# Normalised tiles written in bf16 and transposed in bf16, in the first norm stage of an attention and recurrent-FFN kernel

## The reference

```python
# attention, 16 heads of 64
h = layernorm(x)
q, k, v = h @ w_q, h @ w_k, h @ w_v            # split into heads; q and k are scaled by 1/sqrt(64) each
out = softmax(causal(dot)) @ v
x = x + layernorm(out @ w_u + b_u)
# FFN: a gated recurrence over the first axis (16 steps), then an output layer
c = sigmoid(xt wf + c uf + bf) * c + sigmoid(xt wi + c ui + bi) * tanh(xt wc + c uc + bc)   # xt = layernorm(x)[t]
x = x + layernorm(tanh(xt wo + c_final uo + bo))
```

## Time and profile before

| | us |
|---|---|
| three timed runs | 6600.88, 6709.1, 7143.36 (median 6709.1) |
| the profiled execution | 6599.17 |
| its span on the slowest core | 6597.6 |
| spans of the 8 cores | 6581.2 to 6597.6 |
| granted TensorE clock, mean of a core | 0.781 to 0.786 of full speed |

### The profile page before, as it was taken

The page is one execution under the profiler, slowest core; times in us unless marked ns, Lnnn a source line. Parts: engine busy times, 40 slices in busy tenths (PEclk is TensorE's granted clock), DMA queues, the critical chain, the costliest instruction groups (busy, mean ns, idle before and its releaser), DMA issues.

```text
span 6597.6 us, 85333 instructions; the slowest of 8 cores (6581.2 to 6597.6 us)
## 1 busy us (share of the span) xinstructions
PE 4671.3 (71%) x31972; PEld 2957.2 (45%) x31972; DVE 2211.4 (34%) x4162; ACT 1415.6 (21%) x2602; POOL 486.9 (7%) x399
## 2 busy tenths in 40 slices
PE   4877868686877868686877868687833323999954
PEld 2444444444444444444444444444511113888821
DVE  2232423233232423323242423323222233333378
ACT  1222130413222130413222130413200012222200
POOL 3010100101010100101010100101000011000022
PEclk8878878787878878787887868787855555999976
DMA  5010110101010110101010110101012232000044
GB/s 109 1 61 3 59 40 22 62 1 61 1 61 3 60 45 17 62 1 61 1 61 5 57 52 11 61 1 61 1 61 70 70 115 102 14 14 14 10 148 156
DMA packets 95071, 299.15 MB, mean 45 GB/s; under 512 B 14800, under 2 KB 14800, under 8 KB 94672
## 3 DMA queue, kind: packets, MB, share of 16 engines
q1 hardware_dynamic: 90000, 285.30, 13.1%
q0 software_dynamic: 4672, 8.39, 0.8%
HBM read 268.49 MB, written 33.55 MB: 46 GB/s over the span
## 4 chain that ended last, share of the span: by engine, by line
PE 58%; DVE 14%; ACT 8%; issue 8%; DMA 7%; POOL 3%; SPq 1%; DVEq 0%; ACTq 0%; POOLq 0%
PE PA L445 14%; PE PB L462 13%; PE PB L777 5%; PE PB L523 5%; PE PB L766 5%; ACT ex L559 4%; PE PB L488 3%; PE PA L539 3%; PE PA L324 3%; PE PA L656 3%; DVE of L591 2%; POOL x_ L315 1%; DMA xt<-xg 1%; PE PA L603 1%; PE PB L324 1%
## 5 line engine op out<-in xcount | busy, mean ns | idle before, releaser
L559 ACT ACTIVATE ex<-PA 128x1024 bf16<-128x1024 f32 (+15 forms) x1024 | 623.6, 623 | 2680.0 <-PE PA L549 2637.3
L445 PE MATMUL PA<-lnf,wk_sb 128*128 128x512 bf16 x4096 | 919.4, 389 | 36.4 <-ACT of L335 36.4
L462 PE MATMUL PB<-wv_sb,lnf 128*128 128x512 bf16 x4096 | 886.7, 379 | 0.0
L445 PEld LDWEIGHTS PA<-lnf,wk_sb 128*128 128x128 bf16 x4096 | 407.2, 100 | 547.1 <-issue 86.6
L523 PE MATMUL PB<-ex,va 128*65 128x256 bf16 (+15 forms) x4096 | 482.0, 242 | 206.8 <-ACT ex L559 132.3
L462 PEld LDWEIGHTS PB<-wv_sb,lnf 128*128 128x128 bf16 x4096 | 400.8, 98 | 483.3
L452 DVE CAST kf<-PA 128x512 bf16<-128x512 f32 x512 | 354.0, 691 | 683.9 <-PE PA L445 683.9
L539 PE MATMUL PA<-qf,kf 128*128 128x256 bf16 (+15 forms) x4096 | 509.9, 254 | 22.1 <-DVE qf L499 22.1
L470 DVE CAST va<-PB 128x1024 bf16<-128x1024 f32 x256 | 314.1, 1227 | 578.5 <-PE PB L462 578.5
L584 DVE CAST rb<-PB 64x1024 bf16<-64x1024 f32 x64 | 77.9, 1217 | 1158.8 <-PE PB L577 1158.8
L324 PE MATMUL PA<-identf,lt 128*128 128x128 f32 x640 | 144.4, 401 | 392.0 <-POOL lt L315 311.4
(11 more groups left out here) (116 smaller groups left out, 5182.4 us busy)
## 6 DMA issues: line engine op xcount, KB each, us to landing
xt<-xg SPq DMA_DIRECT2D x128, 512.0 KB, 4.6
xt<-xm SPq DMA_DIRECT2D x96, 512.0 KB, 4.9
ex<-xg SPq DMA_DIRECT2D x64, 512.0 KB, 4.8
of<-xg SPq DMA_DIRECT2D x64, 512.0 KB, 4.5
va<-alns SPq DMA_DIRECT2D x64, 256.0 KB, 5.3
va<-ln2s SPq DMA_DIRECT2D x32, 512.0 KB, 4.2
alns<-ex SPq DMA_DIRECT2D x32, 256.0 KB, 2.0
ln2s<-va SPq DMA_DIRECT2D x16, 512.0 KB, 3.0
```

The lines of the kernel that those rows point to most:

```text
L445: P.op("tensor", lambda t, dmc=dmc, hp=hp, g4=g4, po=po: t.matmul(PA[:, po:po + 512], wk[:, 1024 * dmc + 128 * hp: 1024 * dmc + 128 * (hp ...
L462: P.op("tensor", lambda t, dmc=dmc, kt=kt, hf=hf, po=po: t.matmul(PB[:, po + 512 * hf: po + 512 * (hf + 1)], lnf[:, 2048 * dmc + 128 * kt: ...
L559: P.op("scalar", lambda s, vs=vs, slot=slot, idx=idx: s.activation(sub3(ex, 1024 * (idx % 2) + vs, [256, 4], [1, 256 - vs]), sub3(PA, slot ...
```

## The change

The normalised tile is written in bf16: `lt` (or `x1`) is taken as bf16 and its first 1024 elements used. The transposes read it, with the bf16 identity that the kernel already has, and write bf16 into PSUM, which is taken as bf16 too. With the same column numbers in elements of half the size, a tile takes 2 KB of each partition of PSUM in place of 4 KB, so the two tiles in `PA` lie in its first 4 KB, and those in `PB` likewise. ScalarE's copy reads bf16. Waits, order, loads and counts of instructions are as they were.

```diff
@@ -283,7 +283,7 @@
     par4 = k % nslot
     par2 = k % 2
     xt = slots[par4]
-    lt = B["lt"] if par2 == 0 else B["x1"]
+    lt = (B["lt"] if par2 == 0 else B["x1"]).ap().bitcast(BF16)[:, 0:1024]
     PA = B["PA"]
@@ -313,17 +313,17 @@
     P.wait("gpsimd", "ve_rs")
     P.wait("gpsimd", "te_T", max(P.v("te_T") - 1, 0))
     P.op("gpsimd", lambda g, lt=lt: g.tensor_scalar(
-        lt[:], xt, nm[:, 0:1], rs[:, 0:1], ALU.add, ALU.mult),
+        lt, xt, nm[:, 0:1], rs[:, 0:1], ALU.add, ALU.mult),
         inc="gp_lnapply")
     P.wait("tensor", "gp_lnapply")
     P.wait("tensor", "ve_Tevac", max(P.v("ve_Tevac") - 2, 0))
     pslot = k % 4
-    pbuf = PA if pslot < 2 else B["PB"]
+    pbuf = (PA if pslot < 2 else B["PB"]).ap().bitcast(BF16)
     po = 1024 * (pslot % 2)
     for ch in range(8):
         P.op("tensor", lambda t, ch=ch, po=po, lt=lt, pbuf=pbuf: t.transpose(
             pbuf[:, po + 128 * ch: po + 128 * (ch + 1)],
-            lt[:, 128 * ch:128 * (ch + 1)], B["identf"][:]),
+            lt[:, 128 * ch:128 * (ch + 1)], B["identb"][:]),
             inc="te_T" if ch == 7 else None)
```

## The result

| | us |
|---|---|
| changed kernel, ten timed runs | 6535.59 to 6921.21, median 6545.39 |
| kernel before, ten timed runs beside them | 6596.35 to 7143.36, median 6795.98 |
| ratio, changed to before | 0.9905, 95% interval 0.989 to 0.9919 |

The changed kernel is 0.95% faster, 63 us (6537.9 against 6600.7, medians of the runs that enter the ratio).

A forecast was written before the change was run, and what follows sets the result against it. The norm stage's two-tile ring was taken as the bound; 4.0 + 0.2 + 0.9 = 5.1 us a batch saved, 82 in sixteen, less 7 for the clock at K's start: 6599.2 - 82 + 7 = 6524 us, range 6465 to 6635.

The forecast's parts named there:

- the ring: Norm stage, over two tiles: transposes, copy, Ln, Exp, GpSimd's apply; forecast 5.09 to 4.42 us, remaining the bound; chance 0.6.
- the second one behind it: Norm stage's load loop, four tiles per slot: forecast 8.4 us against 8.84 for the ring; chance that loads bind 0.17.

The follow-up runs named there:

- the last run: Changed kernel with copies waiting for their own transposes, 12 load slots, next batch's first two loads issued early, every bf16 transpose issued twice: 6280.4 to 6289.6 us.

## What to carry to other kernels

Find the ring that sets a stage's pace and the second one behind it, and price the second by what its steps take at the new pace: a load's latency measured at a slow pace is too short. A wait that takes the latest value of a counter can build such a ring out of nothing; correcting the one number gave as much here as halving the length of the transposes. And work taken off TensorE ahead of a dense stage can lower its clock there: compare the matmuls done in the first microseconds, not the busy time.

## What was not expected of the hardware

A stage that holds nothing but transposes, in f32 or bf16, raises the granted clock to 2.4 GHz when long bursts follow each other closely (0.79 and 0.82 on the mean over tile 0 to 14 of one batch); with bf16 bursts of 1.01 us and gaps between them it stayed at 1.2 GHz (0.50) in the norm stages of fifteen batches, in the changed kernel and also at one burst per 1.88 us with twelve slots. The f32 transpose takes two column times for each column at both clocks, bf16 one: eight take 1.94 and 1.07 in f32 and 1.01 in bf16 at 1.2 GHz, and sixteen in bf16 take 1.06 at 2.4 GHz (656.18 to 657.24 in the last run). That the load's time to landing follows its bytes so closely (4.5 for 512 KB, 2.8 for 256 KB), with a load issued every 2.0 to 2.3 us, was not expected either.
